# Cross-attention and quantized feed-forward on one core: keys turned into another bank, a new stage order on every engine, later weight loads

## The reference

```
q      = layernorm(x)                                # 16 heads of 8 features
logits = q.k * 8**-0.5 + b ; positions beyond seq_len masked
x1     = x + softmax(logits) @ v
y      = layernorm(x1)
gate   = silu(bitlinear(y, w_gate)) ; up = bitlinear(y, w_up)     # 128 -> 512
out    = x1 + bitlinear(gate * up, w_down)                        # 512 -> 128
bitlinear(x, w) = act_quant(x) @ weight_quant(w).T   # x: 8-bit steps of the row's peak
                                                     # w: -1, 0 or 1 times mean |w|
```

## Time and profile before

| | |
|---|---|
| median of 3 runs | 195.81 us (195.73 to 196.8) |
| the profiled execution | 195.36 us, its span 193.6 us |
| PE matmul, weight load | busy 150.7 us (78%), 98.0 us (51%) |
| DVE | busy 145.4 us (75%), 709 instructions |
| ACT | busy 142.0 us (73%), 234 instructions |
| POOL | busy 107.1 us (55%), 270 instructions |
| granted PE clock | full until about 177 us, half from there |
| HBM | 7.09 MB read, 2.10 MB written; busy in the first 25 us |

### The profile page before, as it was taken

How to read it: one execution, slowest core, us unless ns; L and a number is a source line. 1 busy time by engine, 2 the same in 40 slices (tenths; PEclk the granted TensorE clock), 3 DMA queues, 4 the chain that set the end, 5 groups by cost and what they waited for, 6 DMA issues and landing times.

```text
span 193.6 us, 6058 instructions
## 1 busy us (share of the span) xinstructions
PE 150.7 (78%) x1842; PEld 98.0 (51%) x1871; DVE 145.4 (75%) x709; ACT 142.0 (73%) x234; POOL 107.1 (55%) x270
## 2 busy tenths in 40 slices
PE   0077888888888888888888888888888888786551
PEld 0043565555565555555565555555566664453241
DVE  2434165788888888888888888888888888999841
ACT  2165988888888888888888888888888887854320
POOL 4155448375757575757575757666665444545120
PEclk9999999999999999999999999999999999998555
DMA  1999950000000000000000000000000000001000
GB/s 30 293 320 325 328 174 5 2 0 5 14 17 14 17 15 14 19 15 19 14 17 14 19 14 17 15 20 14 17 14 17 15 17 14 17 14 32 14 17 27
DMA packets 12944, 9.59 MB, mean 50 GB/s; under 512 B 1008, under 2 KB 12272, under 8 KB 12912
## 3 DMA queue, kind: packets, MB, share of 16 engines
q1 hardware_dynamic: 11424, 8.39, 14.7%
q10 hardware_dynamic: 1488, 0.80, 1.5%
HBM read 7.09 MB, written 2.10 MB: 47 GB/s over the span
## 4 chain that ended last, share of the span: by engine, by line
PE 62%; ACT 15%; DVE 8%; issue 7%; POOL 1%; ACTq 0%; DVEq 0%; POOLq 0%
PE scores L685 18%; PE outs L702 15%; PE turned L760 9%; ACT hqT L572 8%; PE turned L662 7%; PE gates L736 6%; PE ups L772 4%; ACT xqT L555 4%; PE gates L674 2%; ACT probs L538 2%; DVE silu_g L945 1%; DVE h L955 1%; ACT kT L521 1%; DVE stats L895 1%; PE gates L728 1%
## 5 line engine op out<-in xcount | busy, mean ns | idle before, releaser
L538 ACT ACTIVATE probs<-scores,bias_all 128x2048 f32<-128x2048 f32 x32 | 62.8, 1962 | 0.0
L685 PE MATMUL scores<-qT,kT 32*128 32x512 f32 x256 | 37.4, 654 | 1.7 <-ACT probs L538 1.4
L702 PE MATMUL outs<-probs,v_ones 128*32 128x128 f32 x1024 | 34.6, 276 | 0.8 <-issue 0.8
L444 POOL TENSOR_SCALAR hr<-h,h_fac 128x512 f32<-128x512 f32 x32 | 22.0, 689 | 14.4 <-issue 9.2
L662 PE MATMUL turned<-ident_f,q_apart 128*128 128x128 f32 x128 | 20.7, 287 | 11.6 <-POOL q_apart L400 10.4
L702 PEld LDWEIGHTS outs<-probs,v_ones 128*32 128x32 f32 x1024 | 26.1, 109 | 4.6 <-issue 1.9
L426 POOL TENSOR_SCALAR xc<-x_all,neg 128x128 f32<-128x128 f32 x32 | 11.9, 373 | 29.3 <-DVE x_fac L938 28.0
L400 POOL TENSOR_SCALAR q_apart<-x_all,neg,rstd 128x128 f32<-128x128 f32 x32 | 14.2, 443 | 21.2 <-PE turned L662 20.2
L876 DVE RECIPROCAL denom_all<-outs 128x16 f32<-128x16 f32 x32 | 8.2, 258 | 22.6 <-PE outs L717 22.6
L572 ACT ACTIVATE hqT<-turned 128x512 bf16<-128x512 f32 x32 | 19.0, 593 | 8.4 <-PE turned L760 8.4
L521 ACT ACTIVATE kT<-gates 128x128 f32<-128x128 f32 x32 | 8.9, 277 | 22.1 <-PE gates L674 21.9
(11 more groups left out here) (81 smaller groups left out, 275.8 us busy)
## 6 DMA issues: line engine op xcount, KB each, us to landing
ctx_all<-in_ctx SPq DMA_DIRECT2D x1, 2048.0 KB, 14.6
result<-x_all SPq DMA_DIRECT2D x32, 64.0 KB, 1.5
ctx_all<-in_ctx SPq DMA_DIRECT2D x1, 1024.0 KB, 12.2
ctx_all<-in_ctx SPq DMA_DIRECT2D x2, 256.0 KB, 7.6
ctx_all<-in_ctx SPq DMA_DIRECT2D x1, 512.0 KB, 10.3
x_all<-in_x SPq DMA_DIRECT2D x1, 512.0 KB, 10.3
x_all<-in_x SPq DMA_DIRECT2D x2, 128.0 KB, 6.4
w_raw<-in_w_gate ACTq DMA_DIRECT2D x1, 256.0 KB, 7.4
```

The lines of the kernel that those rows point to most:

```text
L444: pool.tensor_scalar(hr[:, p, :], h[:, p, :], h_fac[:, p, :], ROUND, ALU.mult, ALU.add).then_inc(hr_done, 1)
L538: act.activation(probs[:, p, :, :].rearrange("p h q -> p (h q)"), scores[:, :], ACT.Exp, bias=bias_all[:, t.at(k)], scale=SCALE).then_inc( ...
L685: last = pe.matmul(scores[:, 512 * g:512 * (g + 1)], kT[rows, p, :], qT[rows, p, :], start=True, stop=True)
L702: last = pe.matmul(sums_ps[32 * c:32 * (c + 1), 128 * r:128 * (r + 1)], pair[:, 32 * i:32 * (i + 1)], probs[:, p, 2 * (4 * r + c) + i, :], ...
```

## The change

`k_ps`, where turned keys land, moves from gates to ups, with new waits: `k_turn(b)` waits for `finish(b-9)` (before there is one, for `h_product(b-7)`), `project_up(b)` for `k_out(b+6)`, and the wait of `xq_turn` for `k_out` goes. At the start `k_turn(2)`, `(3)`, `(5)` and `(6)` wait for the weights that use ups. The `step` of every engine but SyncE has a new order and new distances. TensorE's scores come one step earlier in its count (`score(b)` in step b+1), the last steps of DVE and POOL are one fewer. The weight loads move from ACT's queue to SP's, behind the first four batches. The core of the diff:

```diff
+K_TURN_AFTER_DOWN = -9
+K_TURN_AFTER_UP = -7
+UP_AFTER_K_TURN = 6
-        k_ps = gates[:, 128:256]
+        k_ps = ups[:, 128:256]
@@ sync: after the loads of batches 2 and 3
+                if i == 1:
+                    sp.dma_start(w_raw[:, GATE, :]...).then_inc(w_in[GATE], 16)
+                    sp.dma_start(w_raw[:, UP, :]...).then_inc(w_in[UP], 16)
+                    sp.dma_start(w_raw[:, DOWN, :], w_down).then_inc(w_in[DOWN], 16)
@@ gpsimd step
-                t.run(h_round, -12)
-                t.run(q_norm, -2)
+                t.run(q_norm, -3)
+                t.once(w_scale_gate, 5)
+                t.run(v_beside_ones, -6)
+                t.run(xc_of, -8)
+                t.run(rstd2_of, -8)
+                t.run(h_round, -11)
+                t.run_pair(rstd1_of, 0)
+                t.run(x_round, -8)
+                t.once(w_scale_down, 4)
                 t.once(w_scale_up, 5)
...
@@ scalar: ahead of the steps, and step
             w_sum_gate()
-            w_sum_up()
+                t.once(w_out_gate, 3)
+                t.once(w_out_down, 6)
+                t.run(q_out, 0)
+                t.run(tanh_of, -6)
+                t.run(sums_of, -3)
+                t.run(k_out, 0)
+                t.once(w_sum_up, 0)
+                t.run(hqT_out, -8)
+                t.run(xqT_out, -5)
+                t.run(weigh, -1)
                 t.once(w_sum_down, 1)
+                t.once(w_out_up, 4)
@@ tensor: k_turn
-                if t.has(k + K_TURN_AFTER_GATE):
-                    pe.wait_ge(silu_done, t.count(k + K_TURN_AFTER_GATE))
+                if t.has(k + K_TURN_AFTER_DOWN):
+                    pe.wait_ge(finished, t.count(k + K_TURN_AFTER_DOWN))
+                elif t.has(k + K_TURN_AFTER_UP):
+                    pe.wait_ge(h_done, t.count(k + K_TURN_AFTER_UP))
+                if t.step + k == 2:
+                    pe.wait_ge(w_meaned, 1)
+                if t.step + k == 3:
+                    pe.wait_ge(w_ready[GATE], 1)
...
@@ tensor: xq_turn, project_up
-                if t.has(k + XQ_AFTER_K_TURN):
-                    pe.wait_ge(kT_done, t.count(k + XQ_AFTER_K_TURN))
+                if t.has(k + UP_AFTER_K_TURN):
+                    pe.wait_ge(kT_done, t.count(k + UP_AFTER_K_TURN))
@@ vector step (the rows below show its order)
-                t.once(w_scales, 5)
+                t.once(w_scales, 4)
```

More of the change, by code:

```diff
@@ L446, in step @@
             def step(t):
[L447 to L458 removed]
+                t.run(q_norm, -3)
[7 more added lines that the diff above has]
+                t.once(w_scale_down, 4)
+                t.once(w_scale_up, 5)
+            run(step, 11)
             def prepare():
@@ L574, in _ @@
             w_sum_gate()
-            w_sum_up()
             def step(t):
-                t.run(k_out, -1)
-                t.once(w_sum_down, 1)
-                t.run(hqT_out, -9)
-                t.run(xqT_out, -6)
-                t.run(weigh, -2)
-                t.run(tanh_of, -6)
-                t.run(q_out, 0)
-                t.run(sums_of, -3)
-                t.once(w_out_gate, 3)
-                t.once(w_out_up, 5)
-                t.once(w_out_down, 6)
-            run(step, 9)
+                t.once(w_out_gate, 3)
[8 more added lines that the diff above has]
+                t.run(weigh, -1)
+                t.once(w_sum_down, 1)
+                t.once(w_out_up, 4)
+            run(step, 8)
             def v_beside_ones(t, k):
@@ L643, in w_turn_down @@
             def w_turn_down():
+                pe.wait_ge(kT_done, 6)
                 pe.wait_ge(w_ready[UP], 1)
@@ L670, in k_turn @@
                     pe.wait_ge(idents, 1)
-                if t.has(k + K_TURN_AFTER_GATE):
-                    pe.wait_ge(silu_done, t.count(k + K_TURN_AFTER_GATE))
+                if t.has(k + K_TURN_AFTER_DOWN):
[3 more added lines that the diff above has]
+                if t.step + k == 2:
+                    pe.wait_ge(w_meaned, 1)
+                if t.step + k == 3:
+                    pe.wait_ge(w_ready[GATE], 1)
+                if t.step + k == 5:
+                    pe.wait_ge(w_ready[UP], 1)
+                if t.step + k == 6:
+                    pe.wait_ge(w_ready[DOWN], 1)
                 arrived(pe, ctx_in, t, k)
@@ L775, in step @@
             def step(t):
-                t.once(w_turn_gate, 4)
-                t.once(w_turn_down, 7)
-                t.run(score, -2)
                 t.run(hq_turn, -9)
-                t.run(k_turn, -1)
+                t.run(sums_turn, -4)
+                t.run(project_up, -7)
                 t.once(w_total_of, 2)
-                t.run(sums_turn, -4)
+                t.run(xq_turn, -6)
+                t.run(q_turn, 0)
+                t.run(project_gate, -6)
                 t.once(w_turn_up, 5)
-                t.run(project_up, -7)
-                t.run(xq_turn, -6)
-                t.run(project_gate, -6)
-                t.run(q_turn, 0)
+                t.once(w_turn_down, 6)
+                t.once(w_turn_gate, 3)
                 t.run(down, -9)
                 t.run(sum_keys, -3)
+                t.run(k_turn, 0)
+                t.run(score, -1)
             run(step, 9)
@@ L1004, in step @@
             def step(t):
+                t.run(attn_of, -8)
                 t.once(range_of, 43)
-                t.run(x_peak_of, -10)
+                t.run(x_peak_of, -9)
+                t.run(x1_of, -8)
+                t.run(h_peak_of, -11)
+                t.run(finish, -13)
+                t.run(h_amp_of, -11)
+                t.run(x_amp_of, -9)
+                t.run(stats2_of, -8)
                 t.run(stats1_of, 0)
-                t.run(denom_of, -9)
-                t.run(h_factor, -13)
+                t.run(x_inv_of, -9)
+                t.run(h_factor, -11)
                 t.run(mean1_of, 0)
-                t.run(attn_of, -9)
-                t.run(h_product, -12)
-                t.run(x1_of, -9)
-                t.run(x_amp_of, -10)
-                t.run(h_peak_of, -12)
-                t.run(stats2_of, -9)
-                t.run(finish, -14)
-                t.run(mean2_of, -9)
-                t.once(w_scales, 5)
-                t.run(x_inv_of, -10)
-                t.run_pair(neg_mean1, 0)
-                t.run(h_amp_of, -12)
-                t.run(neg_mean2, -9)
-                t.run(x_factor, -10)
-                t.run(silu_of, -11)
-            run(step, 14)
+                t.run(mean2_of, -8)
+                t.run(x_factor, -9)
+                t.run(silu_of, -10)
+                t.run(neg_mean2, -8)
+                t.run_pair(neg_mean1, -1)
+                t.once(w_scales, 4)
+                t.run(denom_of, -7)
+                t.run(h_product, -10)
+            run(step, 13)
             verdict_of()
```

22 lines of the change are left out of this document (7 added, 15 removed).

## The result

The changed kernel takes 200.29 us (median of 4 runs, 199.77 to 200.53), the kernel before 196.28 us in the same series. The ratio is 1.020, with a 95% interval of 1.016 to 1.024. The forecast was 193.5 and its range ended at 196.9. The profiled execution took 200.28 us, its span is 198.3 us (before 195.36 and 193.6). So 4.7 us of span are to be explained (by the medians it is 4.0), part by part.

| part | before | after | difference | forecast |
|---|---|---|---|---|
| start, to `score(7)` | 43.33 | 47.90 | +4.6 | +4.4 |
| middle, `score(7)` to `score(31)` | 118.84 | 119.56 | +0.7 | -4.8 |
| end, from `score(31)` | 31.39 | 30.80 | -0.6 | -1.9 |

A forecast was written before the change was run, and what follows sets the result against it. No engine was full (55 to 78%); TensorE's round trip over ScalarE's copies was taken as the bound. Start +3.4 and +1.0, middle -4.8 and end -1.9 gave -2.3 us: forecast 193.5, range 190.2 to 196.9.

The forecast's parts named there:

- The ring: Middle part: the chain through VectorE back to the same stage one step later, 4.74 us; period taken as 4.75, -4.8 us.
- Ring A: Middle part: the chain through ScalarE, from hq_turn over hqT_out, q_turn, down and sum_keys to score, 4.57 us a step.
- rival one: Middle part: Ring A sets the period, 4.57 us, total 189.2; chance 0.12.
- Rival four: Middle part: the period stays at 4.95 us because an unfound wait replaces the old one; total 198.3; chance 0.04.
- Rival three: Middle part: VectorE's new stretch is longer, finish 0.3 late delays k_turn; period 4.90 us, total 197.1; chance 0.14.
- The range: Whole kernel: 190.2 to 196.9 us; the forecast's own range was 191.5 to 195.4, with 0.07 on each step.
- The start: Up to score(7): late weights' sum and GpSimd's queue delay the scores, +3.4 us; score(1) runs slow on TensorE, +1.0.
- Rival two: Start: TensorE stays slow longer, through q_turn(3), weights' transposes, sum_keys(0) and score(2); 2 us more, total 195.5; chance 0.15.
- The loads' move: Start: moving the weight loads costs nothing; bounds -0.5 to +0.5 us.
- The end: From score(31): the range test on VectorE becomes hidden, -1.9 us; other drain steps left as they are, bounds -3 to 0.
- The bank's waits: Middle part: k_turn's new wait for finish is hidden behind sum_keys by some 0.1 to 0.2 us.

The follow-up runs named there:

- The key turn's two runs: Changed kernel with k_turn's transpose issued twice: step 5.100, 203.39 us; changed kernel with k_turn put first in TensorE's next step: step 4.841, 196.4 us.
- the four edits: Changed kernel with the down weights' sum earlier, scalings later, k_turn first in TensorE's step, x_peak_of behind x1_of: 191.76 us, ratio 0.975 to the kernel before.
- the start put right: Changed kernel with the down weights' sum ahead of weigh(0), GpSimd's scalings and the gate weights' turn and copy later: 195.9 us, ratio 0.993 to before.

## Why the prediction was wrong

- **The ring** was the right one, through `h_product`, `attn_of`, `x_peak_of` and `x1_of`, and its size was off: 4.74 forecast, 4.98 measured. The step that failed is the sentence that from `sum_keys` to the next `sums_turn` TensorE has "the same five stages as before, `k_turn` among them, only in another order", with 2.68 as their time. It is 2.84: the order was not free on TensorE, since the key turn's full-width load, put behind the small tiles of `sum_keys`, was exposed and cost 0.15. The key turn's two runs show this part (+0.107 and -0.152 a step). The other 0.08 is read off the rows, not tested: 0.05 at the start of `h_product`, 0.02 at each of the two hand-overs behind it, and -0.01 at the third. Against the 4.75 that was used, 4.98 is 5.5 us over 24 steps, which is the way from -4.8 to +0.7; the one step of 5.25 and the last one of 4.73 cancel.
- **Ring A** was 4.85, not 4.57, for the same reason, so rival one's 189.2 was never within reach. The two rings do stand 0.13 apart, near the 0.15 forecast.
- **Rival four** came nearest in number: a period that stays at 4.95, and 198.3. Its reason was a wait that had not been found. What took most of the gain was no wait for another engine but a weight load on TensorE itself, 0.15 a step.
- **Rival three** named the right kind of failure, a longer stretch, and the wrong place: `k_turn` doesn't wait for `finish` (which ends at 102.44 in the step shown, ahead of 102.70). Its price of 0.15 a step was near by chance. The condition given for a loss, a step over 4.85, held.
- **The range** was too narrow. 0.07 a step was allowed for the ring, and 0.24 came. The prediction said itself that small errors at each hand-over count 24 times.
- **The start** was right in its causes, and in sum (+4.6 for +4.4) with some luck. The sum behind `weigh(0)` cost 2.5, and the queue of GpSimd the rest. The slow clock cost about 1.5 of it, where 1.0 was counted for `score(1)`. Rival two named what lies behind `score(1)`, with 2 us more, and got 0.5; `score(2)` was quick again (1.14 us). The luck: from `score(0)` on it was 5.4 and not 4.4, and 0.8 came back since `score(0)` itself was earlier. The loads' move was counted as nothing. With it alone `score(0)` came 1.0 earlier, and its total didn't change.
- **The end** was forecast at -1.9 with the test's own duration as its price. Its place is worth 1.3 in the changed order (1.2 to 1.6 in the old one); why not the whole 1.9 was not shown. And the drain's other steps, which I left as they are, came up to 0.8 later. Which of the reordered stages makes `h_round(27)` late there was not tried.
- **The bank's waits** hid as forecast in the new order. That the move alone would cost 0.14 a step in the old order was not seen.

## What to carry to other kernels

Where a step is one ring that repeats, each link's error counts once per step, so a forecast of a few per cent needs every hand-over from a row, and the group's order with it: TensorE's time for the same stages in another order was not the same here (2.84 us against 2.68). Look at whose weight load is exposed where the tile shape changes; each such load in front of a full-width stage cost 0.14 or 0.15 us here, so keeping stages of one shape together is worth trying. In a pipelined start ask what each queue holds ahead of the work that everyone waits for, and whether TensorE idles; work of no use in that gap bought about 1% here (ratio 0.990 in the kernel before, and 0.963 for 0.975 with the four edits). Compare starts over several executions: `score(7)` of the same start stood at 43.33 in one with the clock up at 16.9 and at 45.91 in one with 24.5.

## What the runs showed of the hardware that was not expected

- The first full-width transpose behind the 32-column tiles of `sum_keys` cost 0.26 us in the changed kernel, 0.15 of it with its weight load exposed; in the run with the key turn twice, a further transpose behind a full one cost 0.11 in all.
- Executions of one kernel differed by up to 2.9 us (193.67 to 196.53 with the start put right) with nothing else changed. In the profiled ones the clock rose for good at some time from 16.9 to 25.8 us where TensorE was left to idle in the start. In the two kernels with 44 transposes it rose at 8.65 and 7.86, while TensorE had done nothing but transposes.
- The same drain took 31.39 us behind `score(31)` with the fall 15.2 us behind it, and 31.84 with the fall at 13.1.
- On VectorE `x1_of`, which needs the result of `attn_of`, started 0.32 us behind it in the run with `x_peak_of` moved; `x_peak_of`, which doesn't, started 0.20 behind it in the changed kernel.
